# The out-attention's scores in a stack of graph layers: one fp32 matmul, or two fp32r passes over split halves

## The chip, the cores and the metric

The kernel runs on one core of one Trainium2 chip. The metric is the device time of one execution in microseconds (us). The engines are TensorE (PE; its weight loads are listed as PEld), VectorE (DVE), ScalarE (ACT), GpSimd (POOL), and SyncE (SP), whose queue issues most DMAs.

## The reference

x holds 128 graphs of 64 nodes with 512 features. Four layers follow one another, each as x = layernorm(x + layer(x)): a neighbour sum, a graph attention with four heads, an output attention and a feed-forward part (layer 1), and two single-head graph attentions. The change touches the output attention of layer 1 alone, the second call of `_gat_heads` below.

```python
def _gat_heads(x, adj, W, a):
    Wh = jnp.einsum('bnf,hfo->bhno', x, W)
    f1 = jnp.einsum('bhno,ho->bhn', Wh, a[:, :O])
    f2 = jnp.einsum('bhno,ho->bhn', Wh, a[:, O:])
    e = f1[:, :, :, None] + f2[:, :, None, :]
    e = jnp.where(e > 0, e, LEAKY_ALPHA * e)
    e = jnp.where(adj[None, None] > 0, e, NEG_INF)
    attn = jax.nn.softmax(e, axis=-1)
    return jnp.einsum('bhnm,bhmo->bhno', attn, Wh)
...
h = jax.nn.elu(_gat_heads(enc_inputs, adj, W_heads, a_heads))
h = jnp.transpose(h, (0, 2, 1, 3)).reshape(B, N, -1)
out = _gat_heads(h, adj, W_out[None], a_out[None])[:, 0]
out = jax.nn.elu(out)
ffn = jnp.maximum(out @ w1 + b1, 0.0) @ w2 + b2
```

## The kernel before

A tile is 128 rows, two graphs; there are 64 tiles, worked in 32 pairs in layer 1. The large products run as three fp32r passes over operands split into a high and a low half (`split_passes`). The kernel has three stages: layer 0, layer 1 by pairs, and a last stage that runs the feed-forward part and layers 2 and 3 tile by tile.

In layer 1 each engine has a function `step(p)` with its work for one pair in an order written out by hand. `run` calls it for the first pairs, in a hardware loop for most, and for the last ones. A step works on three pairs at once: the projection and aggregation of pair p, the output attention (`ao_`) of pair m = p-1, and the scores of the head-attention (`at`) of pair p+1.

What an attention needs at each graph's nodes is f1 of row i plus f2 of row j. To have one of them along the free dimension, GpSimd makes a diagonal: i64 (the 64x64 identity, twice) times the column f (`pool_diag`, L93 for the out-attention, L203 for the head-attention). TensorE multiplies it by `same_graph`, a 128x128 matrix of ones inside each graph (`pe_scores`, L101 and L212), which spreads each value over the rows of its graph. VectorE adds the other term, applies the leaky slope and the mask (`dve_before_exp`), ScalarE takes the exponential, VectorE the reciprocal of the sum (L248 for the heads, L133 for the out-attention), GpSimd the probabilities (L254, L140), and TensorE turns them (L262, L148).

The head-attention already spreads its scores by two fp32r passes: GpSimd rounds f to fp32r (L196), subtracts to get the low half (L199), and makes a diagonal of both halves (L203). The out-attention's diagonal is one fp32 instruction of 64 columns (L93), and its scores one fp32 matmul (L101).

The order around the two out-attention scores of a pair: TensorE does out_part(p,0,1) (L2083), the scores of tile 2m (even), then an aggregate (L2052); and later the turn of the head-attention (L262), out_part(p,1,2), the scores of tile 2m+1 (odd), out_part(p,1,3). GpSimd does the head-attention's diagonal, one product `products_of` (L1257, 128x512, x times a row, whose sums ScalarE takes at L1396), the even diagonal, another product; and later the head-attention's probabilities, one product, the odd diagonal, three products, the next head-attention diagonal. f comes from VectorE's `out_f` (L1765, L1769), behind which VectorE has the elu of the heads (L1742, L1745); L1751 is the low half of its result. SP loads the x tile of the products (xd) behind the x tile of the aggregate (xa), which waits for the aggregate to be done.

GpSimd's order in `step` is:

```python
if pair(m):
    ao_.pool_prob(nc, pool, 2 * m)
if pair(p + 1):
    at.pool_prob(nc, pool, 2 * p + 3)
if fresh(p + 2):
    products_of(2 * p + 4, p + 2, 0, range(2, 3))
if pair(m):
    ao_.pool_diag(nc, pool, 2 * m + 1, i64)
```

Of the kernel before, what the change touches and what calls it, by code (L numbers as in the profile page):

```python
# [12 lines left out]
P = 128  # L13
# [38 lines left out]
class Attention:  # L52


    def __init__(self, nc, mem, ctx, name, heads, slope, scores_psum, turned_psum, mask=None, f_parts=1):
        def sb(n, shape, dt=F32):
            return mem.enter_context(nc.sbuf_tensor(f"{name}_{n}", shape, dt))

        def sem(n):
            return ctx.enter_context(nc.semaphore(f"{name}_{n}"))  # L60

        self.heads, self.slope, self.mask = heads, slope, mask
        self.f_parts = f_parts
        self.scores_psum = scores_psum
        self.turned_psum = turned_psum
        self.f = sb("f", [P, 2 * heads])
        self.diag = sb("diag", [P, heads, NODES])
        self.e1 = sb("e1", [P, heads, NODES])
        self.e2 = sb("e2", [P, heads, NODES])
        self.ex = sb("ex", [P, heads, NODES])  # L70
        self.peak = sb("peak", [P, heads])
        self.total = sb("total", [P, heads])
        self.inv = sb("inv", [P, heads])
        self.prob = sb("prob", [P, heads, 2, NODES])
        self.turned = sb("turned", [P, heads, P])
        self.pause = sb("pause", [P, 1])
        self.zeroed = sem("zeroed")
        self.f_ready, self.diag_ready, self.scores_done = sem("f_ready"), sem("diag_ready"), sem("scores_done")
        self.summed, self.leaky, self.masked = sem("summed"), sem("leaky"), sem("masked")
        self.peaked, self.exp_ready, self.inverted = sem("peaked"), sem("exp_ready"), sem("inverted")  # L80
        self.prob_ready, self.turned_done, self.turned_ready = (
            sem("prob_ready"), sem("turned_done"), sem("turned_ready"))
# [2 lines left out]

        nc.gpsimd.memset(self.turned[:], 0.0).then_inc(self.zeroed, 1)

    def pool_diag(self, nc, pool, t, i64):

        pool.wait_ge(self.f_ready, self.f_parts * t + (self.f_parts + 1) // 2)  # L90
        ge(pool, self.scores_done, t)
        shape = [P, self.heads, NODES]
        nc.gpsimd.tensor_tensor(self.diag[:], i64[:, None, :].to_broadcast(shape),  # L93
                                self.f[:, 0:self.heads, None].to_broadcast(shape),
                                ALU.mult).then_inc(self.diag_ready, 1)

    def pe_scores(self, nc, pe, t, same_graph):

        pe.wait_ge(self.diag_ready, t + 1)
        ge(pe, self.summed, t)  # L100
        nc.tensor.matmul(self.scores_psum, same_graph[:], self.diag[:].rearrange("p h j -> p (h j)"),  # L101
                         start=True, stop=True).then_inc(self.scores_done, 1)

    def dve_before_exp(self, nc, dve, t, fill):
        shape = [P, self.heads, NODES]
# [55 lines left out]
class HeadAttention:  # L161


    def __init__(self, nc, mem, ctx, name, kept, diag, ones, mask):
        def sb(n, shape, dt=F32):
            return mem.enter_context(nc.sbuf_tensor(f"{name}_{n}", shape, dt))

        def sem(n):
            return ctx.enter_context(nc.semaphore(f"{name}_{n}"))

        self.mask = mask
        self.scores_psum = self.turned_psum = self.prob = None
        self.shape = [P, HEADS, NODES]
        self.f = sb("f", [P, 2, 2 * HEADS])
        self.diag, self.ones = diag[:], ones
        self.e1, self.ex = kept[:, 2], kept[:, 3]
        self.f_halves = sb("f_halves", [P, 2 * HEADS], F32R)
        self.peak = sb("peak", [P, HEADS])
        self.total = sb("total", [P, HEADS])
        self.inv = sb("inv", [P, HEADS])  # L180
        self.turned = sb("turned", [P, 2, HEADS, NODES])
        self.pause = sb("pause", [P, 1])
        self.f_ready = [sem("f_ready0"), sem("f_ready1")]
        self.f_hi_made, self.f_lo_made = sem("f_hi_made"), sem("f_lo_made")
        self.diag_ready, self.scores_done = sem("diag_ready"), sem("scores_done")
        self.summed, self.leaky, self.masked = sem("summed"), sem("leaky"), sem("masked")
        self.peaked, self.shifted, self.exp_ready = sem("peaked"), sem("shifted"), sem("exp_ready")
        self.totalled, self.inverted, self.prob_ready = sem("totalled"), sem("inverted"), sem("prob_ready")
        self.turned_done, self.turned_ready = sem("turned_done"), sem("turned_ready")

    def pool_diag(self, nc, pool, t, p, j, i64):

        pool.wait_ge(self.f_ready[j], 8 * p + HEADS)
        ge(pool, self.scores_done, t)
        hi, lo = self.f_halves[:, 0:HEADS], self.f_halves[:, HEADS:2 * HEADS]
        nc.gpsimd.tensor_tensor(hi, self.f[:, j, 0:HEADS], self.ones[:, 0:HEADS], ALU.mult  # L196
                                ).then_inc(self.f_hi_made, 1)
        pool.wait_ge(self.f_hi_made, t + 1)
        nc.gpsimd.tensor_tensor(lo, self.f[:, j, 0:HEADS], hi.bitcast(F32), ALU.subtract  # L199
                                ).then_inc(self.f_lo_made, 1)  # L200
        pool.wait_ge(self.f_lo_made, t + 1)
        shape = [P, 2 * HEADS, NODES]
        nc.gpsimd.tensor_tensor(self.diag, i64[:, None, :].to_broadcast(shape),  # L203
                                self.f_halves[:, :, None].bitcast(F32).to_broadcast(shape),
                                ALU.mult).then_inc(self.diag_ready, 1)
# [204 lines left out]
def gnn_stack_kernel(nc, x, x_turned, adj, W0T, b0, Wh, ah, Wo, ao, w1, b1, w2, b2, gamma, beta,  # L410
# [16 lines left out]
    with ExitStack() as top:  # L427
        def sb(n, shape, dt=F32):
            return top.enter_context(nc.sbuf_tensor(n, shape, dt))

        def sem(n):
            return top.enter_context(nc.semaphore(n))
# [488 lines left out]
        with ExitStack() as ctx:  # L921
# [59 lines left out]
            def late(n, shape, dt=F32):  # L981
                return ctx.enter_context(nc.sbuf_tensor(n, shape, dt))
# [22 lines left out]
            g2_rows, g2_terms, g2_z = late("g2_v_row", [P, 2, D]), late("g2_terms", [P, 2, D]), late("g2_z", [P, D])  # L1005
            diag_v = [late(f"diag_v{k}", [P, KC, P]) for k in range(2)]
            g2_own, g3_own = late("g2_own", [P, D]), late("g3_own", [P, D])
            still_out, b1_col = late("still_out", [P, 552]), late("b1_col", [P, KC])
            bank_b = hp[0]
            agg_2, agg_3 = (bank.rearrange("p (c n) -> p c n", c=KC) for bank in (agg[:, 0, :], shared[:]))  # L1010
            small_2, small_3 = agg[:, 1, :], smallp[:]
# [229 lines left out]
            def _(pool):  # L1241
# [30 lines left out]
                def step(p):  # L1272
# [13 lines left out]
                        if later(p):  # L1286
                            products_of(2 * p + 3, p + 1, 1, range(6, 7))
                    if pair(m):
                        ao_.pool_diag(nc, pool, 2 * m, i64)
                    if pair(p + 1):  # L1290
                        if later(p):
                            products_of(2 * p + 3, p + 1, 1, range(7, NV))
# [6 lines left out]
                    if fresh(p + 2):  # L1299
                        products_of(2 * p + 4, p + 2, 0, range(2, 3))  # L1300
                    if pair(m):
                        ao_.pool_diag(nc, pool, 2 * m + 1, i64)
                    if fresh(p + 2):
                        products_of(2 * p + 4, p + 2, 0, range(3, 6))
                    if pair(p + 2):
# [60 lines left out]
                pool.wait_ge(h_done, 8 * PAIRS)  # L1366
                pool.wait_ge(at.turned_done, T)
                g3.att.pool_zero(nc)
                ao_.pool_diag(nc, pool, 2 * m, i64)
                ao_.pool_prob(nc, pool, 2 * m)  # L1370
                ao_.pool_diag(nc, pool, 2 * m + 1, i64)
                pool.wait_ge(rows_loaded, 32)
                shift_x1(0, 0)
                ao_.pool_prob(nc, pool, 2 * m + 1)
# [986 lines left out]
```

## Time and profile before

| | us |
|---|---|
| median of 3 runs | 3097.66 (3095.44 to 3099.24) |
| the profiled execution, its own time | 3097.75 |
| its span, first to last instruction | 3096.0 |
| PE busy | 3038.3 (98%) |
| PEld busy | 2656.8 (86%) |
| DVE busy | 2326.0 (75%) |
| ACT busy | 1728.8 (56%) |
| POOL busy | 2110.0 (68%) |

The mean granted clock of TensorE was 0.995 of full speed. Times in the rows below count from the span's start. A matmul's length in them includes its way through the array, so matmuls that follow one another overlap, and the distance between starts tells the pace. TensorE loads the weights of the next matmul while one runs.

### The profile page before, as it was taken

The numbers are of one execution on the slowest core, as the hardware profiler recorded it, in microseconds if no ns is written. First come the engines' busy times: TensorE is split into PE (matmuls) and PEld (weight loads), VectorE is DVE, ScalarE is ACT, GpSimd is POOL, SyncE is SP. The second block draws the span as 40 slices with busy tenths as digits, with TensorE's granted clock in tenths as the row PEclk, the third lists the DMA queues.
The fourth block names the chain that finished last, engine by engine and source line by source line (L and its number), as shares of the span: only waits on it lengthen the run. The fifth ranks groups of instructions, "written<-read, shape, count | busy, mean of one in ns | idle before, by whom it ended". The sixth has DMA issues, their size and how long they took to land.

```text
span 3096.0 us, 65300 instructions
## 1 busy us (share of the span) xinstructions
PE 3038.3 (98%) x19344; PEld 2656.8 (86%) x19344; DVE 2326.0 (75%) x4889; ACT 1728.8 (56%) x4261; POOL 2110.0 (68%) x2901
## 2 busy tenths in 40 slices
PE   8999989999999999999999999999899999999997
PEld 7888868988988888888888888888688888888885
DVE  7777656777777777777777777775788888888885
ACT  3333335555555555555555555553567676676675
POOL 5666635666666666666666666651588888888885
PEclk9999999999999999999999999999999999999999
DMA  5555411112111111111111111112533232233320
GB/s 199 181 187 180 151 54 32 52 44 52 39 54 47 47 54 44 49 43 54 47 47 54 41 49 46 51 48 64 175 96 101 92 102 91 89 102 102 91 75 31
DMA packets 307719, 244.48 MB, mean 79 GB/s; under 512 B 149953, under 2 KB 215489, under 8 KB 307649
## 3 DMA queue, kind: packets, MB, share of 16 engines
q1 hardware_dynamic: 295872, 218.47, 23.7%
q10 hardware_dynamic: 9216, 16.78, 1.4%
q0 software_dynamic: 2560, 8.39, 0.8%
q8 instruction: 32, 0.52, 0.1%
q14 instruction: 39, 0.31, 0.0%
HBM read 159.68 MB, written 83.89 MB: 79 GB/s over the span
## 4 chain that ended last, share of the span: by engine, by line
PE 79%; issue 3%; POOL 3%; DVE 1%; DMA 1%; ACT 0%; SPq 0%; POOLq 0%; ACTq 0%; DVEq 0%
PE hp L2069 23%; PE wop L2083 23%; PE wop L47 9%; PE hp L2227 5%; PE hp L47 5%; PE agg L2052 5%; PE shared L2091 2%; PE agg L2194 2%; PE shared L2194 2%; PE shared L262 1%; POOL g_terms L1325 1%; PE smallp L101 1%; POOL cols L403 0%; PE smallp L212 0%; POOL x1b L1338 0%
## 5 line engine op out<-in xcount | busy, mean ns | idle before, releaser
L1257 POOL TENSOR_TENSOR w_first<-xd,v_row 128x512 f32<-128x512 f32 x480 | 687.2, 1444 | 351.3 <-DMA xd<-x_scratch 275.6
L2069 PE MATMUL hp<-yT_hi,big_hi 128*128 128x256 f32 x2048 | 584.4, 285 | 0.0
L2069 PE MATMUL hp<-yT_hi,big_lo 128*128 128x256 f32 x2048 | 580.6, 283 | 0.0
L2069 PE MATMUL hp<-yT_lo,big_hi 128*128 128x256 f32 x2048 | 580.3, 283 | 0.0
L2083 PE MATMUL wop<-big_hi,hT_hi 128*128 128x512 f32 x1024 | 425.1, 415 | 0.4 <-ACT v_row L1441 0.4
L1751 DVE TENSOR_TENSOR hT_lo<-ex,hT_hi 128x512 fp32r<-128x512 f32 x256 | 268.3, 1048 | 204.3 <-ACT hT_hi L1416 204.3
L2083 PE MATMUL wop<-big_hi,hT_lo 128*128 128x512 f32 x1024 | 402.0, 393 | 0.0
L2083 PE MATMUL wop<-big_lo,hT_hi 128*128 128x512 f32 x1024 | 400.5, 391 | 0.0
L2069 PEld LDWEIGHTS hp<-yT_hi,big_hi 128*128 128x128 f32 x2048 | 393.0, 192 | 5.8 <-DVE yT_lo L1734 0.5
L2069 PEld LDWEIGHTS hp<-yT_lo,big_hi 128*128 128x128 f32 x2048 | 393.0, 192 | 1.9 <-issue 0.7
L2069 PEld LDWEIGHTS hp<-yT_hi,big_lo 128*128 128x128 f32 x2048 | 393.0, 192 | 0.0
L1396 ACT ACTIVATE w_first<-w_first 128x512 f32<-128x512 f32 x480 | 301.6, 628 | 121.0 <-POOL w_first L1257 121.0
L1325 POOL TENSOR_TENSOR g_terms<-x,g_v_row 128x512 f32<-128x512 f32 x256 | 342.4, 1359 | 35.5 <-ACT x L1594 33.8
L1734 DVE TENSOR_TENSOR yT_lo<-agg,yT_hi 128x512 fp32r<-128x512 f32 x256 | 176.2, 688 | 204.1 <-ACT yT_hi L1404 201.5
L1404 ACT CAST yT_hi<-agg 128x512 fp32r<-128x512 f32 x256 | 149.7, 585 | 254.8 <-PE agg L2052 125.2
L2083 PEld LDWEIGHTS wop<-big_hi,hT_hi 128*128 128x128 f32 x1024 | 192.8, 188 | 42.5 <-ACT v_row L1441 0.6
L2083 PEld LDWEIGHTS wop<-big_hi,hT_lo 128*128 128x128 f32 x1024 | 192.3, 188 | 43.0
L47 PE MATMUL wop<-w_hi,g_agg_hi 128*128 128x512 f32 x512 | 220.6, 431 | 4.2 <-DVE g_agg_lo L1895 4.2
L2083 PEld LDWEIGHTS wop<-big_lo,hT_hi 128*128 128x128 f32 x1024 | 193.5, 189 | 31.8
L1411 ACT ACTIVATE ex<-hp 128x512 f32<-128x512 f32 x256 | 152.7, 597 | 99.5 <-PE hp L2069 98.6
L47 PE MATMUL wop<-w_hi,g_agg_lo 128*128 128x512 f32 x512 | 203.4, 397 | 0.0
L47 PE MATMUL wop<-w_lo,g_agg_hi 128*128 128x512 f32 x512 | 202.3, 395 | 0.0
(223 smaller groups left out, 8017.7 us busy)
## 6 DMA issues: line engine op xcount, KB each, us to landing
x0f<-in_x_turned SPq DMA_DIRECT2D x64, 256.0 KB, 2.7
xt<-in_x SPq DMA_DIRECT2D x64, 256.0 KB, 3.0
x_scratch<-w_first ACTq DMA_DIRECT2D x64, 256.0 KB, 2.3
xa<-x_scratch SPq DMA_DIRECT2D x64, 256.0 KB, 2.7
att_hi_scratch<-att_hi SPq DMA_DIRECT2D x64, 256.0 KB, 2.0
att_lo_scratch<-who SPq DMA_DIRECT2D x64, 256.0 KB, 2.0
att_hi<-att_hi_scratch SPq DMA_DIRECT2D x64, 256.0 KB, 3.6
att_lo<-att_lo_scratch SPq DMA_DIRECT2D x64, 256.0 KB, 4.3
```

The costliest lines, as they stand in the source:

```text
L47: ins = nc.tensor.matmul(out, a, b, start=first and c == 0 and q == 0, stop=last and c == n - 1 and q == 2)
L1257: nc.gpsimd.tensor_tensor(terms[:, k % TR, :], xd[:], v_row[:, k, :], ALU.mult).then_inc(terms_ready, 1)
L1325: nc.gpsimd.tensor_tensor(g.terms[:, k, :], x, g.v_row[:, k, :], ALU.mult).then_inc(g.terms_ready, 1)
L1396: nc.scalar.activation(terms[:, k % TR, :], terms[:, k % TR, :], ACT.Identity, accum_out=at.f[:, j, k:k + 1]).then_inc(at.f_ready[j], 1)
L1404: nc.scalar.copy(yT[0][:, side, :, own].rearrange("p c (g n) -> p g c n", g=2), agg[:].rearrange("p g (h c n) -> p h g c n", h=2, c=KC)[:, ...
L1411: nc.scalar.activation(ex[half][:], hp[half][:], ACT.Exp).then_inc(ex_ready, 1)
L1734: nc.vector.tensor_tensor(yT[1][:, side, :, own].rearrange("p c (g n) -> p g c n", g=2), agg[:].rearrange("p g (h c n) -> p h g c n", h=2, ...
L1751: nc.vector.tensor_tensor(hT[1][:, own, :].rearrange("p c n -> p (c n)"), ex[half][:], hT[0][:, own, :].bitcast(F32).rearrange("p c n -> p ...
L2052: ins = nc.tensor.matmul(by_head(agg[:, g, :])[:, :, c, :], xa[j][own, c * P:(c + 1) * P], at.turned[own, j, 2 * q:2 * q + 2, :], start=Tr ...
L2069: ins = nc.tensor.matmul(hp[half][:, s * 2 * P:(s + 1) * 2 * P], a, b, start=c == 0 and i == 0, stop=c == KC - 1 and i == 2)
L2083: ins = nc.tensor.matmul(wop[j][:], a, b, start=h == 0 and c == 0 and i == 0, stop=h == HEADS - 1 and c == KC - 1 and i == 2)
L2227: ins = nc.tensor.matmul(bank[:, s * 2 * P:(s + 1) * 2 * P], x, y, start=c == 0 and q == 0, stop=c == KC - 1 and q == 2)
```

## The change

The out-attention's `pool_diag` rounds f to fp32r, takes the low half, and makes a diagonal of 2x64 columns, as the head-attention does. `pe_scores` multiplies `same_graph` with each half as fp32r, 64 columns each, summed in PSUM. A semaphore (`f_made`) orders the new steps; in the head-attention the two semaphores for its halves become one. The buffers grow, and `still_out`, which keeps the early buffers' room free in the last stage, with them.

```diff
--- before.py
+++ after.py
@@ -64,7 +64,8 @@
         self.scores_psum = scores_psum
         self.turned_psum = turned_psum
         self.f = sb("f", [P, 2 * heads])
-        self.diag = sb("diag", [P, heads, NODES])
+        self.f_halves = sb("f_halves", [P, 2], F32R)
+        self.diag = sb("diag", [P, 2, NODES], F32R)
         self.e1 = sb("e1", [P, heads, NODES])
         self.e2 = sb("e2", [P, heads, NODES])
         self.ex = sb("ex", [P, heads, NODES])
@@ -75,6 +76,7 @@
         self.turned = sb("turned", [P, heads, P])
         self.pause = sb("pause", [P, 1])
         self.zeroed = sem("zeroed")
+        self.f_made = sem("f_made")
         self.f_ready, self.diag_ready, self.scores_done = sem("f_ready"), sem("diag_ready"), sem("scores_done")
         self.summed, self.leaky, self.masked = sem("summed"), sem("leaky"), sem("masked")
         self.peaked, self.exp_ready, self.inverted = sem("peaked"), sem("exp_ready"), sem("inverted")
@@ -85,21 +87,28 @@
 
         nc.gpsimd.memset(self.turned[:], 0.0).then_inc(self.zeroed, 1)
 
-    def pool_diag(self, nc, pool, t, i64):
+    def pool_diag(self, nc, pool, t, i64, ones):
 
         pool.wait_ge(self.f_ready, self.f_parts * t + (self.f_parts + 1) // 2)
         ge(pool, self.scores_done, t)
-        shape = [P, self.heads, NODES]
+        hi, lo = self.f_halves[:, 0:1], self.f_halves[:, 1:2]
+        nc.gpsimd.tensor_tensor(hi, self.f[:, 0:1], ones[:, 0:1], ALU.mult).then_inc(self.f_made, 1)
+        pool.wait_ge(self.f_made, 2 * t + 1)
+        nc.gpsimd.tensor_tensor(lo, self.f[:, 0:1], hi.bitcast(F32), ALU.subtract).then_inc(self.f_made, 1)
+        pool.wait_ge(self.f_made, 2 * t + 2)
+        shape = [P, 2, NODES]
         nc.gpsimd.tensor_tensor(self.diag[:], i64[:, None, :].to_broadcast(shape),
-                                self.f[:, 0:self.heads, None].to_broadcast(shape),
+                                self.f_halves[:, :, None].bitcast(F32).to_broadcast(shape),
                                 ALU.mult).then_inc(self.diag_ready, 1)
 
     def pe_scores(self, nc, pe, t, same_graph):
 
         pe.wait_ge(self.diag_ready, t + 1)
         ge(pe, self.summed, t)
-        nc.tensor.matmul(self.scores_psum, same_graph[:], self.diag[:].rearrange("p h j -> p (h j)"),
-                         start=True, stop=True).then_inc(self.scores_done, 1)
+        for half in range(2):
+            ins = nc.tensor.matmul(self.scores_psum, same_graph[:].bitcast(F32R), self.diag[:, half, :],
+                                   start=half == 0, stop=half == 1)
+        ins.then_inc(self.scores_done, 1)
 
     def dve_before_exp(self, nc, dve, t, fill):
         shape = [P, self.heads, NODES]
@@ -181,7 +190,7 @@
         self.turned = sb("turned", [P, 2, HEADS, NODES])
         self.pause = sb("pause", [P, 1])
         self.f_ready = [sem("f_ready0"), sem("f_ready1")]
-        self.f_hi_made, self.f_lo_made = sem("f_hi_made"), sem("f_lo_made")
+        self.f_made = sem("f_made")
         self.diag_ready, self.scores_done = sem("diag_ready"), sem("scores_done")
         self.summed, self.leaky, self.masked = sem("summed"), sem("leaky"), sem("masked")
         self.peaked, self.shifted, self.exp_ready = sem("peaked"), sem("shifted"), sem("exp_ready")
@@ -194,11 +203,11 @@
         ge(pool, self.scores_done, t)
         hi, lo = self.f_halves[:, 0:HEADS], self.f_halves[:, HEADS:2 * HEADS]
         nc.gpsimd.tensor_tensor(hi, self.f[:, j, 0:HEADS], self.ones[:, 0:HEADS], ALU.mult
-                                ).then_inc(self.f_hi_made, 1)
-        pool.wait_ge(self.f_hi_made, t + 1)
+                                ).then_inc(self.f_made, 1)
+        pool.wait_ge(self.f_made, 2 * t + 1)
         nc.gpsimd.tensor_tensor(lo, self.f[:, j, 0:HEADS], hi.bitcast(F32), ALU.subtract
-                                ).then_inc(self.f_lo_made, 1)
-        pool.wait_ge(self.f_lo_made, t + 1)
+                                ).then_inc(self.f_made, 1)
+        pool.wait_ge(self.f_made, 2 * t + 2)
         shape = [P, 2 * HEADS, NODES]
         nc.gpsimd.tensor_tensor(self.diag, i64[:, None, :].to_broadcast(shape),
                                 self.f_halves[:, :, None].bitcast(F32).to_broadcast(shape),
@@ -1005,7 +1014,7 @@
             g2_rows, g2_terms, g2_z = late("g2_v_row", [P, 2, D]), late("g2_terms", [P, 2, D]), late("g2_z", [P, D])
             diag_v = [late(f"diag_v{k}", [P, KC, P]) for k in range(2)]
             g2_own, g3_own = late("g2_own", [P, D]), late("g3_own", [P, D])
-            still_out, b1_col = late("still_out", [P, 552]), late("b1_col", [P, KC])
+            still_out, b1_col = late("still_out", [P, 624]), late("b1_col", [P, KC])
             bank_b = hp[0]
             agg_2, agg_3 = (bank.rearrange("p (c n) -> p c n", c=KC) for bank in (agg[:, 0, :], shared[:]))
             small_2, small_3 = agg[:, 1, :], smallp[:]
@@ -1286,7 +1295,7 @@
                         if later(p):
                             products_of(2 * p + 3, p + 1, 1, range(6, 7))
                     if pair(m):
-                        ao_.pool_diag(nc, pool, 2 * m, i64)
+                        ao_.pool_diag(nc, pool, 2 * m, i64, ones)
                     if pair(p + 1):
                         if later(p):
                             products_of(2 * p + 3, p + 1, 1, range(7, NV))
@@ -1299,7 +1308,7 @@
                     if fresh(p + 2):
                         products_of(2 * p + 4, p + 2, 0, range(2, 3))
                     if pair(m):
-                        ao_.pool_diag(nc, pool, 2 * m + 1, i64)
+                        ao_.pool_diag(nc, pool, 2 * m + 1, i64, ones)
                     if fresh(p + 2):
                         products_of(2 * p + 4, p + 2, 0, range(3, 6))
                     if pair(p + 2):
@@ -1366,9 +1375,9 @@
                 pool.wait_ge(h_done, 8 * PAIRS)
                 pool.wait_ge(at.turned_done, T)
                 g3.att.pool_zero(nc)
-                ao_.pool_diag(nc, pool, 2 * m, i64)
+                ao_.pool_diag(nc, pool, 2 * m, i64, ones)
                 ao_.pool_prob(nc, pool, 2 * m)
-                ao_.pool_diag(nc, pool, 2 * m + 1, i64)
+                ao_.pool_diag(nc, pool, 2 * m + 1, i64, ones)
                 pool.wait_ge(rows_loaded, 32)
                 shift_x1(0, 0)
                 ao_.pool_prob(nc, pool, 2 * m + 1)
```

## Rows read from the trace of the kernel before

**Rows 1.** Busy time by engine, 550 to 2100 us: busy us and instructions, clock, DMA.
```profile
550.00:2100.00 1550.00, 1547.54 (x11001) 1384.22 (x11000) 1142.93 (x2117) 873.19 (x2156) 1022.07 (x1016) 1.00 0.17 48
```

**Rows 2.** Who waited for whom, weight loads, 550 to 2100: us, times, longest.
```profile
PEld shared L262 <- issue: 10.3, 22, 0.6
PEld smallp L101 <- issue: 10.2, 22, 0.5
```

**Rows 3.** Timeline, TensorE and its weight loads, an odd score at 1493: start, length.
```profile
1493.06 0.40 PE L2083 MATMUL wop<-big_hi,hT_lo 128*128 128x512 f32 x1
1493.51 0.41 PE L101 MATMUL smallp<-ao_diag,same_graph 128*128 128x64 f32 x2
...
1494.04 0.40 PE L2083 MATMUL wop<-big_lo,hT_hi 128*128 128x512 f32 x1
...
1493.48 0.30 PEld L101 LDWEIGHTS smallp<-ao_diag,same_graph 128*128 128x128 f32 x2 [0.46 <-issue]
```

**Rows 4.** Timeline, GpSimd, the diagonal of that score.
```profile
1492.93 0.48 POOL L93 TENSOR_TENSOR ao_diag<-i,ao_f 128x64 f32<-128x64 f32 x1
```

**Rows 5.** Timeline, GpSimd, the next odd diagonal, at 1547.
```profile
1546.51 0.47 POOL L93 TENSOR_TENSOR ao_diag<-i,ao_f 128x64 f32<-128x64 f32 x1
```

**Rows 6.** Timeline, TensorE and its weight loads, that odd score.
```profile
1546.05 0.27 PE L262 MATMUL shared<-ident,ah_prob 128*128 128x128 f32 x1
...
1547.32 0.39 PE L2083 MATMUL wop<-big_hi,hT_lo 128*128 128x512 f32 x1
1547.55 0.33 PE L101 MATMUL smallp<-ao_diag,same_graph 128*128 128x64 f32 x2
...
1548.00 0.40 PE L2083 MATMUL wop<-big_lo,hT_hi 128*128 128x512 f32 x1
...
1547.32 0.42 PEld L101 LDWEIGHTS smallp<-ao_diag,same_graph 128*128 128x128 f32 x2
```

**Rows 7.** Timeline, TensorE, the odd score one pair ahead of rows 3.
```profile
1438.94 0.41 PE L101 MATMUL smallp<-ao_diag,same_graph 128*128 128x64 f32 x2
```

**Rows 8.** Timeline, weight loads, the head-attention's scores in fp32r.
```profile
1510.81 0.30 PEld L212 LDWEIGHTS smallp<-ah_diag,same_graph 128*128 128x128 f32 x2
```

**Rows 9.** The chain that ended last, one piece: start, us, 256-column fp32r matmuls.
```profile
1497.34 5.95 PE hp L2069 x48
```

**Rows 10.** Timeline, GpSimd, the head-attention's halves and diagonal.
```profile
1497.53 0.20 POOL L196 TENSOR_TENSOR ah_f_halves<-ah_f,ones 128x4 fp32r<-128x4 f32 x1
1497.81 0.20 POOL L199 TENSOR_TENSOR ah_f_halves<-ah_f,ah_f_halves 128x4 fp32r<-128x4 f32 x1
1498.09 1.04 POOL L203 TENSOR_TENSOR ah_diag<-i,ah_f_halves 128x512 fp32r<-128x512 f32 x1
```

**Rows 11.** Views of single lines, GpSimd: ns min/median/max, first and last start.
```profile
L93 POOL TENSOR_TENSOR ao_diag<-i,ao_f x64: 292/477/482, 494.0 to 2173.9; 128x64 f32<-128x64 f32 x64
L199 POOL TENSOR_TENSOR ah_f_halves<-ah_f,ah_f_halves x64: 198/203/755, 339.8 to 2069.4; 128x4 fp32r<-128x4 f32 x64
```

**Rows 12.** Timeline, VectorE beside the diagonal of rows 4.
```profile
1491.76 1.50 DVE L1742 TENSOR_SCALAR ex<-ex 128x512 f32<-128x512 f32 x1
1493.29 0.69 DVE L1745 TENSOR_TENSOR ex<-hp,ex 128x512 f32<-128x512 f32 x1
```

**Rows 13.** Timeline, GpSimd, weight loads and VectorE, the even score before rows 3.
```profile
1474.47 0.48 POOL L93 TENSOR_TENSOR ao_diag<-i,ao_f 128x64 f32<-128x64 f32 x1
...
1483.23 3.00 POOL L1257 TENSOR_TENSOR w_first<-xd,v_row 128x512 f32<-128x512 f32 x2 [7.02 <-DMA xd<-x_scratch]
...
1477.85 0.41 PEld L101 LDWEIGHTS smallp<-ao_diag,same_graph 128*128 128x128 f32 x2
...
1483.28 1.79 DVE L1751 TENSOR_TENSOR hT_lo<-ex,hT_hi 128x512 fp32r<-128x512 f32 x1 [0.18 <-ACT hT_hi L1416]
```

**Rows 14.** The chain that ended last, 2150 to 2260, one piece.
```profile
2167.81 7.57 DMA w_second<-in_L_gnn_w
```

**Rows 15.** Timeline, VectorE, L1751 one pair later.
```profile
1537.85 0.69 DVE L1751 TENSOR_TENSOR hT_lo<-ex,hT_hi 128x512 fp32r<-128x512 f32 x1 [0.18 <-ACT hT_hi L1416]
```

## The prediction

> **What bounds the kernel now.** I read the busy times of the layer 1 stretch first, then who waited for whom, then every engine around one pair of scores. From 550 to 2100 us, the loop over the pairs in layer 1 that holds the change, TensorE is busy 1547.54 of 1550 us, at a granted clock of 1.00 [rows 1]. So whatever makes TensorE wait there lengthens the kernel, and whatever it does in less time shortens it. The busy share hides how short the waits are, because the modelled matmul ends overlap them. The view of who waited for whom finds them at the weight loads: before the weight load of the out-attention's scores (L101) the load unit stood idle 22 times for 10.2 us in all, and before the turn of the head-attention's probabilities (L262) 22 times for 10.3 us [rows 2]. The profile calls both "issue", since the semaphore wait is a separate instruction. Their cause is seen by putting engines side by side.
>
> The scores come twice in each pair of tiles: for the even tile (t=2m) before an aggregate, for the odd tile (t=2m+1) between two thirds of an out product. Take the odd one near 1493 us. The last matmul ahead of it starts at 1493.06; in the undisturbed case the next weight load would start with it. Instead it starts at 1493.48 [rows 3]. GpSimd's diagonal (L93) starts at 1492.93 and takes 0.48, so it ends at 1493.41 [rows 4], 0.07 before the load. TensorE waits for GpSimd there. One pair later, at 1547, the diagonal ends at 1546.98 [rows 5] and the load starts with the previous matmul at 1547.32, 0.34 later: no wait [rows 6]. The price of the wait: from the last matmul ahead to the second matmul of the product behind is 1493.06 to 1494.04, 0.98 us, against 1547.32 to 1548.00, 0.68 us: 0.30 us, of a load that is 0.42 us late. The first 0.12 us of lateness is thus free, all beyond goes onto TensorE. This also carries through to the period: odd scores that wait start 54.57 us apart (1438.94 to 1493.51), but the one that doesn't wait comes 54.04 after the last [rows 3, 6, 7]. The difference of 0.53 is the 0.3 lost here and the 0.25 at L262. Nothing later in the loop takes a lost piece back.
>
> **The change, TensorE's part.** One fp32 matmul of 64 columns becomes two fp32r matmuls of 64 columns. In the trace the fp32 one already is two records with two weight loads (0.42 us for the pair of loads, 0.33 for the matmuls) [rows 6], so loads and records stay two. When the scores wait, the two fp32 loads take 0.30 us [rows 3], and so do the two fp32r loads of the head-attention's scores, L212 [rows 8]: one load starts 0.11 after the other, whatever the type. A pass of 64 columns hides behind that: fp32 starts its second 0.06 after its first (0.33 for the two less 0.27 for a single record) [rows 6]. Behind an odd score comes a product with its own load, so only loads count: 0. Behind an even score the aggregate waits for the array to be drained, so the pass's length shows. No row has fp32r at 64 columns. Its nearest row is fp32r at 256 columns, 5.95 us for 48, 0.12 each [rows 9]; the bounds are 0.03 (a quarter of it) and 0.12 (width makes no difference), against 0.06 now. That is -0.03 to +0.06 for each of 31 even scores, -0.9 to +1.9 us; I take 0, between them. The removal of half the array's work buys nothing, because the weight loads set the pace.
>
> The Trainium skill's page "TensorE: Matmul & The Clock Gate", section "LDWEIGHTS (loading the stationary operand)", gives columns/1.2 for a load, 107 ns for 128; the trace's 0.11 agrees. Its page "FP8 and Floating Point Precision", section "TensorE Precision Notes", says that true fp32 needs four passes; going by passes alone one would book a gain on all scores, which is a rival below.
>
> **The change, GpSimd's part.** Ahead of each diagonal come two small instructions, each waiting for the one before, and the diagonal doubles from 64 to 128 columns. The same three steps stand in the head-attention's pool_diag [rows 10]: first half at 1497.53, second at 1497.81, diagonal at 1498.09. So each small one costs 0.28 us of path, 0.20 of work and 0.08 of waiting. The diagonal's width: 64 columns take 0.292 undisturbed [rows 11] and 512 take 1.04 [rows 10], which is 1.67 ns a column, and 0.11 us for 64 more. Sum: 0.28 + 0.28 + 0.11 = **0.67 us later**. L93's 0.48 in place of 0.29 [rows 4, 11] is not in that sum: VectorE's L1742 runs until 1493.26 [rows 12] and holds the diagonal back by 0.19; now it will hold the first half back by the same, and L1745, VectorE's next [rows 12], reads PSUM and only one SBUF tile; I take it to be no hindrance. The low bound is 0.56 (the wider diagonal free), the high one is with VectorE in the way: the second half of the head-attention took up to 0.755 in place of its median 0.203 [rows 11]; 0.43 of that, somewhat under the whole 0.55, makes 1.1 us.
>
> The Trainium skill's page "SBUF — State Buffer", section "SBUF: two separate sides", explains such lengthening by a port pair that VectorE and GpSimd hold one at a time for a whole instruction. That fits the 0.19; it would make new collisions possible, and they are in the high bound.
>
> **What lies beside other work.** Even tiles: the diagonal ends at 1474.95 and its load starts at 1477.85, 2.90 us later [rows 13]; 0.67 is covered. The product behind it (L1257) moves by 0.67 too, but GpSimd then stands idle 7.02 us for the next x tile [rows 13], whose DMA is queued on SP behind one that waits for TensorE's aggregate. Behind an odd diagonal GpSimd's products, and through them the next head-attention diagonal, come 0.67 later; that diagonal ends at 1499.13 and its load starts at 1510.81 [rows 8, 10], and TensorE itself has moved as far. The merging of two semaphores into one adds at most register work on a queue that runs ahead: 0.
>
> **What lies on the path.** Odd tiles in the loop: 27 (t=5 to 57). The 22 that wait [rows 2] pay in full: 22 x 0.67 = 14.7 us. The other 5 are like the one at 1547: its load could start 0.07 after the diagonal, so there is 0.34 - 0.07 = 0.27 of slack; 0.67 - 0.27 = 0.40 late, less the free 0.12, is 0.28: 5 x 0.28 = 1.4 us. The two odd tiles ahead of the loop (t=1, 3) lie between the two kinds: 2 x 0.5 = 1.0. The last odd tiles, and the even one in the tail at 2167.6, I take at 0: the chain that ended last runs there through the load of w2 from 2167.81 for 7.57 us [rows 14]. Bounded above by 0.67 each, 2 us. Sum: 14.7 + 1.4 + 1.0 = **+17.1 us**. On the profiled execution's 3097.75 that is 3114.8; the median of the runs, 3097.66, is 0.1 from it. **Forecast 3114.8 us, 0.55% slower.**
>
> **Rivals.** (a) *Not slower: a race tips.* What makes 22 of 27 odd tiles wait is that GpSimd's product starts 0.05 before VectorE's L1751 (1483.23 against 1483.28), which then takes 1.79 us; where VectorE was first it took 0.69 [rows 13, 15], its chain came about 1 us sooner, and neither L262 nor L101 waited. If the change delays that product by over 0.1 us, all 27 tip: 27 x 0.28 = 7.6 in place of 22 x 0.53 = 11.7, with the 1.0 of the start -3.1 us: 3094.7. Against it: the product waits for a DMA that TensorE releases, not GpSimd. 9%. (b) *The slip is absorbed*, by another wait later in the loop that shrinks: near 3099. The periods of 54.57 and 54.04 speak against it. 4%. (c) *The halves collide* with VectorE: 1.1 in place of 0.67 adds 0.43 to each of 29: 12.5 us, 3127.3. 12%. (d) *Passes count*: the 0.06 between the fp32 records is saved at 62 scores, 3.7 us, while the diagonal is as late as above: 3111.1; 4%, and inside the range.
>
> **How the numbers follow.** The forecast's case has 71%: 3104 to 3122, by the bounds of 0.56 (-2.9 us) and of the even scores (-0.9 to +1.9), and by how many odd tiles happen to win the race (each one more wins back 0.67 + 0.53 - 0.28 = 0.9 us; ten more are 9 us). The range 3104 to 3129 takes in (c) and (d) and leaves out (a), (b) and the tails. A measurement of this kernel tells about 0.2% from no change, 6.2 us: faster would be below 3091.5, which needs (a) and a gain on TensorE: 3%. Within 0.2%: (a) and (b), 10%. Slower: 87%.
>
> **What would show it.** The diagonal's instructions beginning at product's end with two 0.20 ones 0.28 apart, and a diagonal of 0.40; at odd scores the weight load 0.07 behind the diagonal and about 1.09 behind the matmul ahead (now 0.42), in all or nearly all of 27; idle time before L101's loads near 22 x 1.13 + 5 x 0.4 = 27 us in place of 10.2; before L262's unchanged; periods near 55.2. Even scores with no wait. I am wrong if the idle time at L262 goes (the race tipped), if the diagonal's second half takes over 0.5, or if the first half runs before the product ends.

## The result and the profile after

Both medians are of five runs; the table of the kernel before calls the same median one of three.

| | before | after |
|---|---|---|
| median of 5 runs, us | 3097.66 (3095.44 to 3099.24) | 3115.77 (3113.08 to 3116.4) |
| span of the profiled execution, us | 3096.0 | 3114.6 |

The change makes the kernel 0.56% slower: the ratio is 1.0056, with a 95% interval of 1.0044 to 1.0069. The forecast was 3114.8 us, 0.55% slower.

The page of the changed kernel, busy us by engine. TensorE's busy time hardly moves (3038.3 before), GpSimd's rises from 2110.0:

```profile
span 3114.6 us, 65624 instructions
...
PE 3037.9 (98%) x19344; PEld 2651.6 (85%) x19344; DVE 2304.9 (74%) x4889; ACT 1740.0 (56%) x4261; POOL 2154.1 (69%) x3029
```

TensorE has as many instructions as before, 19344 matmul records and as many weight loads. GpSimd has 128 more (3029 in place of 2901), two for each of 64 tiles.

Who waited for whom at the weight loads, 550 to 2100 us, of the changed kernel (engine, tile and line, us in total, times, longest). Every such view below is of the same stretch. L109 is the out-attention's scores (L101 before), L271 the turn of the head-attention (L262 before), to be read against rows 2:

```profile
PEld smallp L109 <- issue: 29.3, 28, 1.1
...
PEld shared L271 <- issue: 11.3, 25, 0.5
```

The idle time before the scores' loads has gone from 10.2 to 29.3 us, by 19.1, about the whole rise of the span (18.6). The waits at the turn went from 10.3 to 11.3 us, and from 22 to 25.

The timeline of TensorE and its weight loads around the same odd score as in rows 3, now at 1505 us:

```profile
1503.92 0.39 PE L2092 MATMUL wop<-big_hi,hT_lo 128*128 128x512 f32 x1
1505.03 0.38 PE L109 MATMUL smallp<-ao_diag,same_graph 128*128 128x64 f32 x2 [0.72 <-issue]
...
1505.56 0.40 PE L2092 MATMUL wop<-big_lo,hT_hi 128*128 128x512 f32 x1
...
1505.00 0.30 PEld L109 LDWEIGHTS smallp<-ao_diag,same_graph 128*128 128x128 f32 x2 [1.11 <-issue]
```

The timeline of GpSimd (POOL) and VectorE (DVE) beside it:

```profile
1502.12 1.73 POOL L1266 TENSOR_TENSOR w_first<-xd,v_row 128x512 f32<-128x512 f32 x1
1503.81 0.37 POOL L95 TENSOR_TENSOR ao_f_halves<-ao_f,ones 128x1 fp32r<-128x1 f32 x1
1504.26 0.19 POOL L97 TENSOR_TENSOR ao_f_halves<-ao_f,ao_f_halves 128x1 fp32r<-128x1 f32 x1
1504.53 0.40 POOL L100 TENSOR_TENSOR ao_diag<-i,ao_f_halves 128x128 fp32r<-128x128 f32 x1
...
1502.63 1.50 DVE L1751 TENSOR_SCALAR ex<-ex 128x512 f32<-128x512 f32 x1
1504.16 0.69 DVE L1754 TENSOR_TENSOR ex<-hp,ex 128x512 f32<-128x512 f32 x1
```

The diagonal ends at 1504.93, and the weight load starts 0.07 behind it, as in [rows 3, 4]. From the start of the first instruction behind the product to the diagonal's end it is now 1.12 us, in place of 0.48 [rows 4]: 0.64 more. From the last matmul ahead to the second behind it is 1.64 us, where it was 0.98 [rows 3].

The even score of that pair, the counterpart of rows 13 (weight loads, matmuls, GpSimd, VectorE):

```profile
1488.75 0.41 PEld L109 LDWEIGHTS smallp<-ao_diag,same_graph 128*128 128x128 f32 x2
...
1488.97 0.30 PE L109 MATMUL smallp<-ao_diag,same_graph 128*128 128x64 f32 x2
...
1486.09 0.40 POOL L100 TENSOR_TENSOR ao_diag<-i,ao_f_halves 128x128 fp32r<-128x128 f32 x1
...
1494.10 1.29 POOL L1266 TENSOR_TENSOR w_first<-xd,v_row 128x512 f32<-128x512 f32 x1 [6.36 <-DMA xd<-x_scratch]
...
1494.19 1.75 DVE L1760 TENSOR_TENSOR hT_lo<-ex,hT_hi 128x512 fp32r<-128x512 f32 x1 [0.21 <-ACT hT_hi L1425]
```

This diagonal is ready at 1486.49, 2.26 us before its load, so its later coming is covered. The product still waits for its DMA, now 6.36 us.

### The profile page after: what moved, and what is told of

Same layout as the page of the kernel before. It is cut to its first block, busy times and chain, and to the rows that moved or that the text cites. A ratio compares the mean times of both kernels' runs of the same rounds, so it can differ in the third digit from the quotient of the medians.

```text
span 3114.6 us, 65624 instructions
## 1 busy us (share of the span) xinstructions
PE 3037.9 (98%) x19344; PEld 2651.6 (85%) x19344; DVE 2304.9 (74%) x4889; ACT 1740.0 (56%) x4261; POOL 2154.1 (69%) x3029
## 4 chain that ended last, share of the span: by engine, by line
PE 78%; issue 4%; POOL 3%; DVE 1%; DMA 1%; ACT 0%; SPq 0%; POOLq 0%; ACTq 0%; DVEq 0%
PE hp L2078 23%; PE wop L2092 22%; PE wop L47 9%; PE hp L2236 5%; PE hp L47 5%; PE agg L2061 5%; PE shared L2100 2%; PE agg L2203 2%; PE shared L2203 2%; PE shared L271 1%; POOL g_terms L1334 1%; PE smallp L109 1%; POOL cols L412 0%; PE smallp L221 0%; DMA xd<-x_scratch 0%
## 5 line engine op out<-in xcount | busy, mean ns | idle before, releaser
L1760 DVE TENSOR_TENSOR hT_lo<-ex,hT_hi 128x512 fp32r<-128x512 f32 x256 | 245.9, 961 | 205.3 <-ACT hT_hi L1425 205.3
L1334 POOL TENSOR_TENSOR g_terms<-x,g_v_row 128x512 f32<-128x512 f32 x256 | 342.6, 1359 | 35.6 <-ACT x L1603 33.9
L1751 DVE TENSOR_SCALAR ex<-ex 128x512 f32<-128x512 f32 x256 | 154.4, 603 | 70.0 <-ACT ex L1420 69.9
```

The lines of the kernel that those rows point to most:

```text
L1334: nc.gpsimd.tensor_tensor(g.terms[:, k, :], x, g.v_row[:, k, :], ALU.mult).then_inc(g.terms_ready, 1)
L1751: nc.vector.tensor_scalar(ex[half][:], ex[half][:], 1.0, -1.0, ALU.min, ALU.add).then_inc(neg_ready, 1)
L1760: nc.vector.tensor_tensor(hT[1][:, own, :].rearrange("p c n -> p (c n)"), ex[half][:], hT[0][:, own, :].bitcast(F32).rearrange("p c n -> p ...
```

## The experiments

Each ratio compares a run with the kernel before, run beside it on the same chip. The groups were run on different chips, where the kernel before itself came out between 3096.9 and 3098.0 us; a difference in us between two groups is good to 1 or 2 us. The theory is the prediction's: TensorE's part is worth nearly nothing, and GpSimd's three steps ahead of the odd diagonal are paid in full where TensorE already waited.

### TensorE's part alone, and GpSimd's part alone

`pe_only` makes the diagonal in one step, and sets its second half to zero once, at the start:

```diff
...
-        nc.gpsimd.tensor_tensor(hi, self.f[:, 0:1], ones[:, 0:1], ALU.mult).then_inc(self.f_made, 1)
-        pool.wait_ge(self.f_made, 2 * t + 1)
-        nc.gpsimd.tensor_tensor(lo, self.f[:, 0:1], hi.bitcast(F32), ALU.subtract).then_inc(self.f_made, 1)
-        pool.wait_ge(self.f_made, 2 * t + 2)
-        shape = [P, 2, NODES]
-        nc.gpsimd.tensor_tensor(self.diag[:], i64[:, None, :].to_broadcast(shape),
-                                self.f_halves[:, :, None].bitcast(F32).to_broadcast(shape),
+        nc.gpsimd.tensor_tensor(self.diag[:, 0:1, :], i64[:, None, :].to_broadcast([P, 1, NODES]),
+                                self.f[:, 0:1, None].to_broadcast([P, 1, NODES]),
                                 ALU.mult).then_inc(self.diag_ready, 1)
```

> TensorE's part of the change alone: GpSimd makes the diagonal with one instruction of 64 columns, as before, and TensorE runs the two fp32r matmuls. Left out: the low half of f (its columns are a constant zero), so scores have f rounded to fp32r. Theory (the slowdown is GpSimd's diagonal coming later at odd tiles): odd weight loads wait about as often and as long as before (22 times, 10 us), each even score is 0.025 us shorter, 0.8 us in all: 3096.9 us, ratio 0.9997. Rival (the fp32r passes or the changed buffers and semaphores cost the time): 3110 or more, ratio 1.004 or above.

Measured: 3096.23 us, ratio 0.9996 (0.9986 to 1.0005). `pool_only` keeps GpSimd's steps and gives TensorE one matmul:

```diff
-        for half in range(2):
-            ins = nc.tensor.matmul(self.scores_psum, same_graph[:].bitcast(F32R), self.diag[:, half, :],
-                                   start=half == 0, stop=half == 1)
-        ins.then_inc(self.scores_done, 1)
+        nc.tensor.matmul(self.scores_psum, same_graph[:], self.diag[:, 0, :].bitcast(F32),
+                         start=True, stop=True).then_inc(self.scores_done, 1)
```

> GpSimd's part of the change alone: the two halves and the 128-column diagonal are made, but TensorE runs one fp32 matmul over the high half's 64 columns. Left out: the low half is made but not added. Theory: idle time before these weight loads 27 to 30 us as after the change, 0.8 us more on even scores: 3116.6 us, ratio 1.006. Rival (TensorE's part costs the time): 3098, ratio 1.000.

Measured: 3115.36 us, ratio 1.0053 (1.0037 to 1.0070). The waits at the scores' weight loads, of `pe_only` and then of `pool_only`:

```profile
PEld smallp L106 <- issue: 11.1, 24, 0.5
```

```profile
PEld smallp L108 <- issue: 28.9, 28, 1.1
```

The slowdown comes with GpSimd's part and goes with it. The two fp32r passes, the larger buffers and the merged semaphores, which `pe_only` has too, cost nothing that can be measured.

### The odd tiles alone, and the even tiles alone

Both keep a second, fp32 diagonal buffer of 64 columns, and use the old form for one tile of each pair. The edit of the odd tiles alone, against the changed kernel:

```diff
+        if not split:
+            nc.gpsimd.tensor_tensor(self.diag_whole[:], i64[:], self.f[:, 0:1].to_broadcast([P, NODES]),
+                                    ALU.mult).then_inc(self.diag_ready, 1)
+            return
...
-                        ao_.pe_scores(nc, pe, 2 * m, same_graph)
+                        ao_.pe_scores(nc, pe, 2 * m, same_graph, split=False)
```

> The change at odd tiles alone; even tiles keep the fp32 matmul and the 64-column diagonal in a buffer of their own. The computation is whole. Theory: the odd diagonals carry all: 3116.2 us, ratio 1.006. Rival (both tiles of a pair share in it, since GpSimd's queue is later after both): about 3107, ratio 1.003.

> The change at even tiles alone. The computation is whole. Theory: their diagonal is ready over 2 us before its weight load even when 0.67 us later, and the pass is 0.025 us shorter: 3096.9 us, ratio 0.9997, with 22 or so waits before odd loads as before. Rival (both tiles share): about 3107, ratio 1.003.

Measured: odd tiles alone 3114.79 us, ratio 1.0054 (1.0038 to 1.0071); even tiles alone 3096.49 us, 0.9998 (0.9989 to 1.0008). The same instructions added at the even tiles are free, and at the odd ones they cost the whole difference. The two places differ by their cover: over 2 us at one, none at the other. The waits at the scores' loads say the same, odd alone first. L118 is the matmul of the split form, L114 that of the old one, so both rows are of odd tiles:

```profile
PEld smallp L118 <- issue: 29.2, 28, 1.1
```

```profile
PEld smallp L114 <- issue: 11.5, 25, 0.5
```

### The price of one step

`wide_only` takes the two small instructions out and leaves the 128-column diagonal:

```diff
-        nc.gpsimd.tensor_tensor(hi, self.f[:, 0:1], ones[:, 0:1], ALU.mult).then_inc(self.f_made, 1)
...
-        nc.gpsimd.tensor_tensor(lo, self.f[:, 0:1], hi.bitcast(F32), ALU.subtract).then_inc(self.f_made, 1)
...
-                                self.f_halves[:, :, None].bitcast(F32).to_broadcast(shape),
+                                self.f[:, 0:1, None].to_broadcast(shape),
```

> The changed kernel without the two small instructions: the diagonal has 128 columns, both halves of it the whole f. Left out: the split, so the scores hold f twice. Theory (each step of GpSimd ahead of the odd load is paid by its own length): 0.11 us at some 27 odd tiles, 3.0 us, less 0.8 at the even ones: 3099.5 us, ratio 1.0007, idle time before the odd loads 13 to 14 us. Rival (the doubled diagonal is the costly part): 3110 or more.

Measured: 3100.55 us, ratio 1.0007 (0.9998 to 1.0017). `third_small` adds one more:

```diff
...
+        nc.gpsimd.tensor_tensor(hi, self.f[:, 0:1], ones[:, 0:1], ALU.mult).then_inc(self.f_made, 1)
+        pool.wait_ge(self.f_made, 3 * t + 2)
...
```

> The changed kernel with one more small GpSimd instruction in the chain: the first half is made twice, one after the other. Theory: 0.28 us at 29 odd tiles, 8.1 us more than the changed kernel: 3123.9 us, ratio 1.0087, idle time before the odd loads about 37 us. Rival (what TensorE waits for is something else by now, the slip saturates): under 3119.

Measured: 3123.74 us, ratio 1.0083 (1.0068 to 1.0099), 8.0 us over the changed kernel's 3115.77. GpSimd's timeline in `third_small` and the weight load behind it:

```profile
1509.01 0.37 POOL L95 TENSOR_TENSOR ao_f_halves<-ao_f,ones 128x1 fp32r<-128x1 f32 x1
1509.46 0.19 POOL L97 TENSOR_TENSOR ao_f_halves<-ao_f,ones 128x1 fp32r<-128x1 f32 x1
1509.72 0.19 POOL L99 TENSOR_TENSOR ao_f_halves<-ao_f,ao_f_halves 128x1 fp32r<-128x1 f32 x1
1509.99 0.40 POOL L102 TENSOR_TENSOR ao_diag<-i,ao_f_halves 128x128 fp32r<-128x128 f32 x1
...
1510.46 0.30 PEld L111 LDWEIGHTS smallp<-ao_diag,same_graph 128*128 128x128 f32 x2 [1.37 <-issue]
```

The steps are 0.26 and 0.27 us apart, 0.19 of it work. 29 of them are 7.7 us, against the 8.0 between the medians and 7.9 of idle time before the scores' loads (37.2 in place of 29.3). A small dependent instruction is paid at the odd tiles one for one. For the wide diagonal alone (`wide_only`) the time is too near that of the kernel before to be told from it, and the idle time carries the reading. It was expected at 13 to 14 us, and was 15.4:

```profile
PEld smallp L104 <- issue: 15.4, 27, 0.6
...
PEld shared L266 <- issue: 11.8, 27, 0.5
```

Each wait is as forecast. The timeline of GpSimd and of the weight load in `wide_only`:

```profile
1493.70 0.58 POOL L95 TENSOR_TENSOR ao_diag<-i,ao_f 128x128 fp32r<-128x128 f32 x1
...
1494.36 0.30 PEld L104 LDWEIGHTS smallp<-ao_diag,same_graph 128*128 128x128 f32 x2 [0.57 <-issue]
```

The diagonal takes 0.58 us in place of the 0.48 of [rows 4], both held back by VectorE, and the load stands idle for 0.57 in place of 0.46 [rows 3]: 0.11 more. The 15.4 us come from the count: in this run all 27 odd tiles of the loop waited. How many do is a race, taken up below.

### More cover for the odd load

The same edit on both kernels moves the odd scores one step back in TensorE's order:

```diff
                     if pair(p):
                         out_part(p, 1, 2)
+                        out_part(p, 1, 3)
                     if pair(m):
                         pe.wait_ge(ao_.turned_ready, 2 * (2 * m + 1))
                         ao_.pe_scores(nc, pe, 2 * m + 1, same_graph)
-                    if pair(p):
-                        out_part(p, 1, 3)
```

> The changed kernel, with the odd scores one step later in TensorE's order: behind the last third of the out product instead of ahead of it, 1.4 us more of cover. Theory: the weight load then comes when the diagonal has been ready or is at most 0.1 us late, so the waits of 29 us before it vanish, 25 x 0.97 plus a little: 3090.5 us, ratio 0.9977. Rival (the lateness is only handed on, through softmax and turn, to the next turn and out sums, which have 1.6 us of cover): 3105 or more, with new waits at L148 or behind it.

> The kernel before, with the same move of the odd scores. Theory: 22 waits of 0.30 us go, 6.6 us: 3091.1 us, ratio 0.9979, and within 1.5 us of the changed kernel with the same move. Rival (the change costs something beside that wait): the changed kernel with the move stays 5 us or more above this one.

Measured: the changed kernel with it 3088.99 us, ratio 0.9973 (0.9964 to 0.9983); the kernel before with it 3088.03 us, 0.9973 (0.9964 to 0.9982). In both, the view of the weight loads' waits has no row left for the scores. That of the changed kernel:

```profile
PEld agg L2061 <- issue: 20.1, 57, 0.4
PEld shared L271 <- issue: 10.9, 25, 0.5
```

This is the sharpest of the tests: with cover for GpSimd's 0.64 us, the two forms of the scores are within 1 us of each other, and both are faster than the kernel before. Beside that one wait the change costs nothing that can be measured. The out-attention's softmax now begins 1.4 us later, and the view shows no new wait behind it.

### Who goes first, GpSimd's product or VectorE's subtraction

The prediction had it from [rows 13, 15] that odd tiles wait where GpSimd's product starts just ahead of VectorE's L1751 (L1760 after). One added wait forces the other order:

```diff
                     if fresh(p + 2):
+                        pool.wait_ge(hT_lo_ready, 8 * p + 4)
                         products_of(2 * p + 4, p + 2, 0, range(0, 2))
```

> The kernel before with the same added wait. Theory: all 27 pairs as the 5 without a wait, 22 x 0.53 = 11.7 us less: 3086.0 us, ratio 0.9962. Rival: 3098 or more, the wait costs GpSimd 0.7 us a pair and gives nothing.

> The changed kernel, GpSimd's first product of the next even tile (L1266) made to wait until VectorE's L1760 ahead of the head scores is done, so VectorE always goes first there. Theory: L1760 takes 0.69 us in all pairs, the waits at L271 vanish, the odd diagonal comes 0.95 us sooner and its load is 0.4 us late with 0.28 lost, in all 27 pairs: 3097.7 - 11.7 + 7.4 + 1.0 - 0.8 = 3093.6 us, ratio 0.9987. Rival (the order of the two doesn't set the waits): 3115 or more.

Measured: the kernel before with it 3084.63 us, ratio 0.9963 (0.9950 to 0.9976), as expected. The changed kernel with it 3101.94 us, 1.0018 (1.0009 to 1.0027): some 13 us below the changed kernel, but 8.3 us above what was expected. The waits before the turn are gone in both, so the mechanism holds. What was mis-sized is how much sooner VectorE gets through. The timeline of the changed kernel with the wait, VectorE and GpSimd:

```profile
1484.60 0.69 DVE L1761 TENSOR_TENSOR hT_lo<-ex,hT_hi 128x512 fp32r<-128x512 f32 x1 [0.20 <-ACT hT_hi L1426]
...
1485.72 1.38 DVE L234 SCALAR_TENSOR_TENSOR w_first<-w_first 128x256 f32<-128x256 f32 x1
...
1485.53 2.73 POOL L1266 TENSOR_TENSOR w_first<-xd,v_row 128x512 f32<-128x512 f32 x2 [7.37 <-DVE hT_lo L1761]
...
1494.36 0.40 POOL L100 TENSOR_TENSOR ao_diag<-i,ao_f_halves 128x128 fp32r<-128x128 f32 x1
...
1494.83 0.30 PEld L109 LDWEIGHTS smallp<-ao_diag,same_graph 128*128 128x128 f32 x2 [0.81 <-issue]
```

and the kernel before, VectorE, in a pair where the product came first:

```profile
1485.50 1.01 DVE L225 SCALAR_TENSOR_TENSOR w_first<-w_first 128x256 f32<-128x256 f32 x1
```

The product, held back until 1485.53, now lies beside VectorE's next instruction with two inputs in SBUF, which takes 1.38 in place of 1.01 us. (Even 1.01 isn't its clear length: the shortest of its 57 in the kernel before took 0.47.) Of the time won, 0.37 us is lost again, and the odd load comes some 0.76 us late, not 0.40. The pairs paid 0.64 instead of 0.28 each; 27 x 0.36 = 9.7 us, near the 8.3 that the time is above its expectation. The kernel before with the wait has the same collision, 1.39 us in place of 1.01:

```profile
1474.37 1.39 DVE L225 SCALAR_TENSOR_TENSOR w_first<-w_first 128x256 f32<-128x256 f32 x1
```

There it uses up the 0.27 us of slack of a pair that had won the race, and the odd load is late in every pair, but little: 0.17 us of idle time. Its waits at the scores, in place of 10.2 us in 22 waits in the kernel before as it was:

```profile
PEld smallp L101 <- issue: 4.9, 28, 0.3
```

### Both remedies

> The changed kernel with both remedies: the odd scores behind the last third of the out product, and GpSimd's product behind VectorE's L1760. In the run with the second remedy alone the odd loads stayed 0.76 us late; 1.4 us of cover takes that in. Theory: no wait before L109's nor before L271's loads: 3097.0 - 11.7 - 0.8 = 3084.5 us, ratio 0.9959. Rival (the move's softmax now comes late for the turn): 3090 or more, waits at the turn.

> The kernel before with both remedies. Theory: no waits either, and 0.8 us above the changed kernel with both, for the fp32 passes at even tiles: 3085.3 us, ratio 0.9962; no gain over the added wait alone (3084.6), which had left 0.05 us a pair. Rival (the change's extra GpSimd work costs beside that wait): 5 us or more below the changed kernel with both.

The two edits together, on either kernel. Measured: the changed kernel with both 3082.61 us, ratio 0.9952 (0.9938 to 0.9965); the kernel before with both 3083.70 us, 0.9951 (0.9937 to 0.9964). They were expected at 3084.5 and 3085.3. In the changed kernel with both, only the wait of the aggregate is left, which every version has:

```profile
PEld agg L2062 <- issue: 20.1, 57, 0.4
```

This version beats the kernel before by 15 us and the changed one by some 32. Between the two forms the changed one is 1.1 us ahead, where 0.8 was expected from the passes. But the ratios are equal within their intervals, so the times don't show which form is faster.

## Why the prediction was right

**TensorE waits for the odd diagonal.** Shown, by the load 0.07 behind the diagonal before and after, by the odd and even tiles alone, and by the moved scores.

**The price of GpSimd's steps.** Forecast 0.67 us, measured 0.64. The small steps took 0.27 each where nothing stood in their way. The diagonal took 0.40, 0.11 over the undisturbed 0.292 [rows 11], as the prediction had worked out. The first half took 0.37, held back by VectorE's L1751 by as much as the old diagonal was; L1754, the instruction behind it, hindered neither the second half nor the diagonal. The collision of rival (c) didn't happen.

**How many tiles pay.** Forecast 22 in full and 5 in part. 25 paid in full: that many had a wait before the turn, in place of 22 [rows 2]. Three more pairs lost the race, at 0.53 + 0.64 us each 3.5 us, where their share was forecast as 3 x 0.28. This is the step that was mis-sized, by 2.7 us, and it made the kernel slower than forecast; the smaller 0.64 took back 0.7. The sum by measured terms: 22 x 0.64 = 14.1, three pairs 3.5, two pairs in part 0.7, the two ahead of the loop 1.0, less 0.6 to 0.8 at even scores: 18.5 to 18.7, against 18.6 of span. Nothing shows that the change sets the number: the loads at the turn waited 24 times with TensorE's part alone and with GpSimd's part alone, 25 with the even tiles alone, 25 in the kernel before with the odd scores moved, and 27 with the wide diagonal alone. Whether a kernel keeps its number from one execution to the next was not tried, so what sets it stays open.

**What the sum leaves out.** Its terms end with the loop, and the span doesn't. The even score at the loop's end (tile 58) has its load at 2075.93 before and 2095.24 after, 19.3 us later. 0.4 of that was there at the very first score (498.24 and 498.62), before any wait for a diagonal. Behind the loop the even score in the tail (tile 62), which the prediction took at nothing, has its load at 2167.61 and 2187.59, 20.0 later, and GpSimd's first long instructions of the last stage (L1325, L1334 after) start at 2190.58 and 2210.47, 19.9 later. The last stage, whose instructions the change doesn't touch, gives 1.3 us back, and 18.6 are left. No experiment says why. So the mechanism and the 0.64 are shown, but that the forecast lies within 1 us of the median is in part luck: the race (+2.7), the smaller step (-0.7), the passes (-0.6 to -0.8) and these ends offset one another in part.

**TensorE's part.** Forecast 0, between -0.9 and +1.9 us. The pair of records takes 0.30 in place of 0.33 [rows 6], so the pass of 64 columns costs 0.03, the low bound. From the last matmul ahead of an even score to the aggregate's first is 0.46 us in place of 0.48 or 0.49, as the starts show (1488.74 to 1489.20, and 1477.85 to 1478.34 before). Over 31 even scores the passes are worth some -0.6 to -0.8 us. At odd tiles the loads set the pace: 0.30 us for the two, before and after [rows 3]. Rival (d), that passes count at all scores, falls with that: the time by it would have been saved at the even ones alone.

**The slip is not absorbed.** Odd scores that wait are 55.20 us apart, 1449.83 to 1505.03, against 54.57 [rows 3, 7]: 0.63 more, or all of the 0.64. The line of the earlier one, of the changed kernel:

```profile
1449.83 0.38 PE L109 MATMUL smallp<-ao_diag,same_graph 128*128 128x64 f32 x2 [0.70 <-issue]
```

**The race does not tip.** Rival (a) had the product delayed. It starts 0.09 before L1760 (1494.10 and 1494.19), as it was 0.05 before [rows 13], since it waits for a DMA behind TensorE's aggregate. The experiments show that the race matters (12 us in the kernel before), and the change doesn't delay the product there: what it does to the count is within what the variants show among themselves.

The Trainium skill's page "SBUF — State Buffer", section "SBUF: two separate sides", has the loser of the shared port pair wait for the winner's whole instruction. It counts VectorE's instructions with two inputs in SBUF among those that take part. The runs agree, nearly to the length: L1760 takes 0.69 us ahead of a product (as L1761 in the timeline above) and 1.75 behind one, 1.06 longer, where the product had 1.20 still to run. And L1754, which reads PSUM and one SBUF tile, lay beside GpSimd's second half without lengthening it; in all 64 tiles that half took 0.191 to 0.194 us.

## What to carry to other kernels

Before a matmul is made cheaper at the price of work on another engine, look at which engine its weight load waits for: the same 0.64 us was free where the operand was 2.9 us early, and was paid in every pair where it was already late. In this profile such a wait is easily missed, since TensorE looks 98% busy, and it shows as "issue" at the load, with the true releaser ending 0.07 us ahead on another engine's timeline. Moving the consumer back by one independent block made both versions faster here, by 0.27%, and no new wait came of it.

## What the runs showed of the hardware

An fp32r pass of 64 columns starts the next record 0.03 us later, an fp32 one 0.06; both forms need two weight loads, 0.11 us from one to the next, and so cost TensorE the same at the odd scores, where the loads are not hidden. A chained one-column GpSimd instruction costs 0.27 us, 0.19 of work and 0.08 of handing on. And a product that was held back to let one VectorE instruction pass landed on the next one: of the 1.1 us won, 0.37 was lost so.
